# Last mixture-of-experts layer: tokens grouped before the experts, four experts a tile instead of eight

## What is computed

```python
flat = layernorm(h) * ln_scale + ln_bias              # 8768 x 128
out_shared = swiglu(flat @ shared_in_w.T) @ shared_out_w.T + shared_out_b
g_idx = argmax(flat @ group_gate_w.T + group_bias)    # one of 2 groups for each token
e_sel = expert logits of that group + bias            # 4 logits
e_probs = softmax(e_sel); topv, topi = top_k(e_probs, 2); topv /= topv.sum() + 1e-8
comb, cnt = zeros(S, 8), zeros(S, 8)                  # topv and 1.0 at g_idx*4 + topi
h_expert = swiglu(flat @ expert_in_w.T)               # 8768 x 256, the same for all experts
routed = cnt @ expert_out_bias
for e in range(8):
    routed += comb[:, e:e+1] * (h_expert @ expert_out_weight[e].T)
h = h + out_shared + routed
```

## Time and profile before

| | us |
|---|---|
| median of three runs | 1777.07 (1775.9 to 1777.42) |
| the profiled execution, its own time | 1775.86 |
| its span, first to last instruction | 1773.9 |
| `last_norm` | about 1345 to 1393 |
| `mix_experts` | 1393.98 to the end |
| mean granted clock of TensorE over the span | 0.902 |

### The profile page before, as it was taken

How to read it: one execution, slowest core, us unless ns; L and a number is a source line. 1 busy time by engine, 2 the same in 40 slices (tenths; PEclk the granted TensorE clock), 3 DMA queues, 4 the chain that set the end, 5 groups by cost and what they waited for, 6 DMA issues and landing times. The chain is left out here.

```text
span 1773.9 us, 27554 instructions
## 1 busy us (share of the span) xinstructions
PE 1388.5 (78%) x9068; PEld 992.5 (56%) x9068; DVE 1134.5 (64%) x1837; ACT 677.5 (38%) x1150; POOL 800.8 (45%) x833
## 2 busy tenths in 40 slices
PE   5679999999873332876727848888998699999998
PEld 3567777777542221765625623333334478887877
DVE  2755555555367782211114888888885889888998
ACT  3234444444443321322203548787875311111111
POOL 1455445444320034888865237777743333232331
PEclk9889999999985565999867969999999899999999
DMA  4070000000001032544443000000001000000000
GB/s 168 1 289 15 0 0 0 0 0 0 0 1 26 1 102 64 100 78 86 78 106 128 1 2 2 1 0 0 0 1 40 1 9 13 13 13 13 9 13 17
DMA packets 56803, 61.75 MB, mean 35 GB/s; under 512 B 15507, under 2 KB 46577, under 8 KB 55425
## 3 DMA queue, kind: packets, MB, share of 16 engines
q1 hardware_dynamic: 40835, 49.69, 8.6%
q0 software_dynamic: 13888, 10.24, 4.2%
q10 hardware_dynamic: 2016, 1.00, 0.2%
HBM read 36.49 MB, written 25.59 MB: 35 GB/s over the span
## 5 line engine op out<-in xcount | busy, mean ns | idle before, releaser
L1946 PE MATMUL at_slot<-at_qm,at_ks 128*128 128x512 bf16 (+1 forms) x640 | 160.3, 384 | 19.5 <-DVE at_clip L2151 10.2
L502 PE MATMUL ga_kv<-ga_kern,ga_v 128*128 128x274 f32 x512 | 133.5, 403 | 13.5 <-ACT ga_kern L591 12.6
L2667 DVE TENSOR_REDUCE mx_routed<-mx_weighted 128x128 f32<-128x1024 f32 x69 | 138.1, 2001 | 2.4
L2625 POOL TENSOR_TENSOR mx_h_E<-mx_hid_E,mx_h_E 128x768 fp32r<-128x768 f32 x23 | 43.5, 1890 | 188.8 <-DVE mx_h_E L2657 188.8
L84 PE MATMUL mx_e<-ff_expert_out_high,mx_h_E 128*128 128x512 f32 x276 | 112.3, 407 | 10.7 <-DVE mx_weighted L2664 10.7
L2030 ACT ACTIVATE at_clip<-at_slot,at_four 128x1024 bf16<-128x1024 f32 (+1 forms) x96 | 106.9, 1113 | 32.1 <-PE at_slot L1946 30.3
L1429 POOL DMA_INDIRECT moe_sums<-ex_y,slot_sums x69 | 108.4, 1570 | 22.4 <-issue 20.3
L2151 DVE TENSOR_SCALAR at_clip<-at_slot 128x1024 bf16<-128x1024 f32 (+1 forms) x96 | 116.1, 1218 | 3.1 <-PE at_slot L1946 2.8
L502 PEld LDWEIGHTS ga_kv<-ga_kern,ga_v 128*128 128x128 f32 x512 | 92.2, 189 | 37.8 <-ACT ga_kern L591 16.8
L85 PE MATMUL mx_e<-ff_expert_out_low,mx_h_E 128*128 128x512 f32 x276 | 109.6, 397 | 0.0
L653 POOL TENSOR_TENSOR ga_rot<-ga_by_cos,ga_by_sin 128x274 f32<-128x274 f32 x64 | 48.6, 759 | 134.9 <-DVE ga_by_sin L697 134.9
(11 more groups left out here) (457 smaller groups left out, 3835.9 us busy)
## 6 DMA issues: line engine op xcount, KB each, us to landing
moe_sums<-ga_zeros SPq DMA_DIRECT2D x8, 1152.0 KB, 13.4
ar_rows<-moe_sums SPq DMA_DIRECT2D x34, 256.0 KB, 3.9
ex_down<-in_down SPq DMA_DIRECT2D x32, 192.0 KB, 2.5
token_rows<-ct_rows SPq DMA_DIRECT2D x17, 256.0 KB, 2.4
out_h<-H SPq DMA_DIRECT2D x22, 192.0 KB, 1.9
H<-in_text SPq DMA_DIRECT2D x1, 4096.0 KB, 21.4
patches<-in_patches SPq DMA_DIRECT2D x1, 1728.0 KB, 8.2
ga_sin<-in_sin SPq DMA_DIRECT2D x1, 1644.0 KB, 7.9
```

What stands on the lines that cost most here:

```text
L502: last = nc.tensor.matmul(kv[:, e, 0:HALF], v[p][:, mt + 2 * side, e * P:(e + 1) * P], kern[(p + g) % 2][:, side, :], start=mt == 0 and si ...
L1946: last = nc.tensor.matmul(to[r0:r0 + r, g % 2, :].rearrange("p (s n) -> p s n", s=2), ks[m][:, t * P:t * P + r], qm[m][:, 2 * g:2 * g + 2, ...
L2667: nc.vector.tensor_reduce(R[p][t][:], weighted[:].rearrange("p e d -> p d e"), AX.X, ALU.add).then_inc(reduced, 1)
```

## The change

The last layer is split in two phases.

`last_norm` gains one DMA: a DRAM table `by_group` of 70 x 128 rows of 133 floats (4.77 MB) is filled with zeros from an input of the same size, and SyncE waits for it before it leaves the block.

`route()` also works out for each token a row of that table: tokens of the first group count up from the front, tokens of the second group count down from the back, with at least 64 blank rows between, so that every tile of 128 rows holds one group only. TensorE counts the tokens that come earlier (`rank`), and turns all 69 tiles of `F` to rows (`stage_turn`); ScalarE copies them to `stage` (`keep_stage`), beside four expert weights and the token's number. GpSimd scatters the rows of each tile to the table, 69 indirect DMAs.

Phase 1, beside the scatter, still goes by 23 chunks of 384 tokens and does only the shared feed-forward and the expert biases. Its output is turned to rows (`turn_rows`, `keep_rows`) and stored to the output, which is now 8768 x 128. Phase 2 reads the table back, 18 chunks of 4 tiles (the last of 2), turns the rows, does the experts' hidden layer 512 tokens at a time, and for each tile only the four experts of its group: 6 matmuls of 512 columns, whose column offset is worked out in a register. VectorE weighs and adds the four results with four operations on 128 x 128, each of which needs the one before. GpSimd adds the rows to the output by an indirect DMA that accumulates, 70 in all. GpSimd does no arithmetic in `mix_experts` any more; VectorE makes all low parts. The loops are unrolled.

The core of the diff, new lines only where an old one is told above:

```diff
@@ last_norm, sync
+            sp.dma_start(grouped_d, x["blank"]).then_inc(blanked, 16)
...
+            sp.wait_ge(blanked, 16)
@@ mix_experts, sync
+            for c in range(CHUNKS):
+                sp.wait_ge(rows_out, c + 1)
...
+                sp.dma_start(out[at:at + whole * P, :].rearrange("(t p) d -> p t d", p=P), rows[c % 2][:, 0:whole, :]).then_inc(stored[c % 2], 16)
...
+            sp.wait_ge(grouped, 1)
+            for c, (t, n) in enumerate(CHUNKS2):
+                if c >= LOADS:
+                    sp.wait_ge(weighed, CHUNKS2[c - LOADS][0] + CHUNKS2[c - LOADS][1])
+                sp.dma_start(tiles[c % LOADS][:, 0:n, :],
+                             grouped_d[t * P:(t + n) * P, :].rearrange("(t p) d -> p t d", p=P)).then_inc(loaded[c % LOADS], 16)
@@ mix_experts, tensor
+            def project(c):
+                pe.wait_ge(hidden, c)
                 pe.wait_ge(f_low, c + 1)
...
+            def experts(c, i, first_count):
+                j = CHUNKS2[c][0] + i
+                if i == 0:
+                    pe.wait_ge(h_low2, c + 1)
+                if j >= 2:
+                    pe.wait_ge(weighed, j - 1)
+                tokens = slice(i * P, (i + 1) * P)
+                at = (((P * j + BEYOND - first_count) >> BEYOND_BITS) & 1) * 512
...
+            project(0)
+            for g in range(EARLY):
+                stage_turn(g)
+            rank()
+            for g in range(EARLY, len(FGROUPS)):
+                stage_turn(g)
+            turn_cnt(0)
+            for c in range(CHUNKS):
+                if c + 1 < CHUNKS:
+                    project(c + 1)
+                finish(c)
+                if c + 1 < CHUNKS:
+                    turn_cnt(c + 1)
+                if c > 0:
+                    turn_rows(c - 1)
+            turn_rows(CHUNKS - 1)
+            first_count = nc.tensor.value_load(boundary[0:1, 0:1], min_val=0, max_val=NT)
+            pe.wait_ge(rows_out, CHUNKS)
+            turn(0)
+            turn(1)
+            project2(0)
+            for c, (t, n) in enumerate(CHUNKS2):
+                for i in range(n):
+                    experts(c, i, first_count)
+                    if i == 0 and c < LAST2:
+                        project2(c + 1)
+                    if i == 1 and c + 2 <= LAST2:
+                        turn(c + 2)
@@ mix_experts, gpsimd
+            for t in range(TILES):
+                if t % 4 == 0:
+                    pool.wait_ge(staged, t // 4 + 1)
+                nc.gpsimd.indirect_dma_start(out=grouped_d, out_offset=bass.IndirectOffsetOnAxis(ap=place_i[:, t:t + 1], axis=0),
...
+            for j in range(GTILES):
+                pool.wait_ge(weighed, j + 1)
+                nc.gpsimd.indirect_dma_start(out=out, out_offset=bass.IndirectOffsetOnAxis(ap=ids[:, j:j + 1], axis=0),
+                                             in_=R[j % RING], in_offset=None, bounds_check=NT - 1, oob_is_err=False,
+                                             compute_op=ALU.add).then_inc(sent[j % RING], 16)
@@ mix_experts, vector
+            def weigh(c, i):
+                j = CHUNKS2[c][0] + i
+                dve.wait_ge(expert_done, j + 1)
+                if j >= RING:
+                    dve.wait_ge(sent[j % RING], 16 * (j // RING))
...
+                nc.vector.tensor_scalar(r, part(0), share(0), None, ALU.mult).then_inc(acc, 1)
+                for e in range(1, 4):
+                    accs[0] += 1
+                    dve.wait_ge(acc, accs[0])
+                    nc.vector.scalar_tensor_tensor(r, part(e), share(e), r, ALU.mult, ALU.add).then_inc(acc if e < 3 else weighed, 1)
...
+            tokens(0)
             route()
+            tokens(1)
+            hide(0)
+            for c in range(CHUNKS):
+                if c + 1 < CHUNKS:
+                    hide(c + 1)
+                if c + 2 < CHUNKS:
+                    tokens(c + 2)
+                add(c)
...
+            for c, (t, n) in enumerate(CHUNKS2):
+                for i in range(n):
+                    weigh(c, i)
+                    if i == 1 and c < LAST2:
+                        hide2(c + 1, 0)
+                        high_at[c + 1] = accs[0]
+                    if i == min(2, n - 1) and c < LAST2:
+                        hide2(c + 1, 1)
+                    if i == min(2, n - 1) and c + 2 <= LAST2:
+                        tokens_low2(c + 2)
```

More of the change, by code:

```diff
@@ L51 @@
 NEX = 8
+GT = 4
+GCH = GT * P
+GTILES = -(-(NT + P - 1) // P)
+GROW = P + 5
+BEYOND_BITS = 14
+BEYOND = 1 << BEYOND_BITS
+ID_BIAS = 20000
 BIAS_ROWS = NE + EXPAND // P
@@ L2464, in _, with mix_experts @@
                 turn(n)
-def mix_experts(nc, k, H, F, GL, high, low, out):
+def mix_experts(nc, k, x, H, F, GL, high, low, grouped_d, out):
     with ExitStack() as st:
@@ L2515, in _ @@
+        from_front, to_back, token_id = (order[:, P + n * TILES:P + (n + 1) * TILES] for n in (1, 2, 3))
+        ones = order[:, P + 4 * TILES:]
+        FGROUPS = [(t, min(4, TILES - t)) for t in range(0, TILES, 4)]
+        EARLY = 4
+        CHUNKS2 = [(t, min(GT, GTILES - t)) for t in range(0, GTILES, GT)]
+        LAST2 = len(CHUNKS2) - 1
         @block.sync
         def _(sp):
-            with sp.Fori(0, CHUNKS - 1) as c:
-                sp.wait_ge(added, 2 * c + 3)
-                sp.sem_inc(met, 1)
-                sp.dma_start(out[:, bass.ds(c * CH, CH)], H[:, bass.ds(c * CH, CH)]).then_inc(stored, 16)
@@ L2521, in _ @@
-            sp.wait_ge(added, 2 * (CHUNKS - 1) + 3)
-            sp.dma_start(out[:, (CHUNKS - 1) * CH:NT], H[:, (CHUNKS - 1) * CH:NT]).then_inc(stored, 16)
-            sp.wait_ge(stored, 16 * CHUNKS)
+            sp.dma_start(order[:], x["order"]).then_inc(order_in, 16)
+            for c in range(CHUNKS):
+                sp.wait_ge(rows_out, c + 1)
+                whole = min(CT, (NT - c * CH) // P)
+                at = c * CH
+                sp.dma_start(out[at:at + whole * P, :].rearrange("(t p) d -> p t d", p=P), rows[c % 2][:, 0:whole, :]).then_inc(stored[c % 2], 16)
+                rest = min(CH, NT - at) - whole * P
+                if rest:
+                    sp.dma_start(out[at + whole * P:NT, :], rows[c % 2][0:rest, whole, :]).then_inc(stored[c % 2], 16)
@@ L2590, in _, with turn_cnt, finish @@
-            loop(pe, body)
-            finish(CHUNKS - 1, 0)
+            def turn_cnt(c):
+                if c == 0:
+                    pe.wait_ge(counted, 3)
+                    pe.wait_ge(staged, len(FGROUPS))
+                else:
+                    pe.wait_ge(cnt_out, c)
+                for t in range(CT):
+                    last = nc.tensor.transpose(t_ps[0][0:NEX + 1, t * P:(t + 1) * P], cnt[:, CT * c + t, :], k["ident"][:])
+                last.then_inc(cnt_ps, 1)
+            def finish(c):
+                pe.wait_ge(h_low, c + 1)
+                pe.wait_ge(placed_at if c < 2 else added, 1 if c < 2 else c - 1)
+                for f in range(2):
+                    split_matmul(nc, e_ps[c % 2][:, 0:CH], (high["shared_out"][:, f, :], low["shared_out"][:, f, :]),
+                                 [part[:, f, 0:CH] for part in h[c % 2]], f == 0, False)
+                pe.wait_ge(cnt_out, c + 1)
+                nc.tensor.matmul(e_ps[c % 2][:, 0:CH], high["out_bias"][:], cnt_t[:], start=False, stop=False)
+                nc.tensor.matmul(e_ps[c % 2][:, 0:CH], low["out_bias"][:], cnt_t[:], start=False, stop=True).then_inc(y_done, 1)
@@ new lines, in project2 @@
+            def project2(c):
+                n = CHUNKS2[c][1] * P
+                pe.wait_ge(hidden2, c)
+                pe.wait_ge(f_low2, c + 1)
+                for ps, at in ((a_ps, 0), (b_ps, 2)):
+                    for f in range(2):
+                        cols = slice((at + f) * P, (at + f + 1) * P)
+                        last = split_matmul(nc, ps[:, f, 0:n], (high["expert_in"][:, cols], low["expert_in"][:, cols]),
+                                            [part[:, 0:n] for part in f_parts[c % 2]], True, True)
+                last.then_inc(projected2, 1)
@@ new lines, in experts @@
+            def experts(c, i, first_count):
[6 more added lines that the diff above has]
+                at = (((P * j + BEYOND - first_count) >> BEYOND_BITS) & 1) * 512
+                for f in range(2):
+                    cols = bass.ds(at, 512)
+                    last = split_matmul(nc, e_ps[j % 2][:], [part[:, f, tokens] for part in h[c % 2]],
+                                        (high["expert_out"][:, f, cols], low["expert_out"][:, f, cols]), f == 0, f == 1)
+                last.then_inc(expert_done, 1)
@@ L2849, in _arrays @@
     a["owner"] = np.stack([~late, late], 1).astype(f)
+    token = np.arange(NTP).reshape(TILES, P).T
+    real = token < NT
+    front = np.where(real, token, 1 << 20)
+    back = np.where(real, GTILES * P - 1 - token, 0)
+    above = np.zeros((P, TILES))
+    above[:TILES] = np.arange(TILES)[:, None] < np.arange(TILES)[None]
```

(2 more changed lines are left out.)

367 lines of the change are left out of this document (195 added, 172 removed).

## The result

The changed kernel takes 1841.7 us, the median of four runs (1836.9 to 1842.2), beside 1777.2 us of the kernel before on the same chip: a ratio of 1.0358, with an interval of 1.0340 to 1.0377. The direction was forecast and the size was not: +64 us where the chain gave +26.

A forecast was written before the change was run, and what follows sets the result against it. TensorE (96.8% busy) and VectorE (90.4%), both nearly full, bound the last stage; a chain of fill, route, 23 chunks, handover, 18 chunks and end, with 2 us for cold starts, gave a span of 1800, hence 1803; range 1772 to 1842.

The forecast's parts named there:

- the chain: Whole span: fill, route, 23 chunks, handover, 18 chunks, end; 1800 against 1773.9, so 1803; 1790 to 1826 had 0.55.
- Removed and added work, and the transfers: Last stage: 12 matmuls a tile become 6, reductions vanish; fill 11.6 us and scatter 129 us, both hidden.
- Route and phase 1: From routing to the last `hide`: first `hide` at 1415, 21 rounds of 6.9 us, 145 us, last at 1564.
- Handover: Between the phases: from last `hide` to first expert matmul at 1584, 20 us in which no engine is full.
- Phase 2, the step that failed: Experts' phase: rounds of 12.2 us (bounds 11.3 and 14), 16 rounds 195 us, the short one 9.3.
- TensorE's clock: Both phases: new gaps of 2.5 and about 3 us lie near the 2.59 us wait, so full clock is kept.
- a part of it: Cold bursts in part: a quarter of phase 2's bursts gives +23, 1826; half of all +69, 1872; called likelier.
- the whole burst at half clock: Cold-bursts rival, both phases: 2.0 and 5.5 us a round, 137 us, 1940; colder or dearer rounds above 1826 had 0.20.
- The offset: Phase 2's round: 12.1 us taken as 12.2 for register work on the column offset, which no row prices.
- End: After the last chunk starts at 1788.5: last two tiles and last scatter, about 9 us, to 1797.7.
- VectorE's own rate: Rival, phase 2: weigh 1 not held up by TensorE's order, 10.1 us a chunk, 1769; 0.14, shared with other shorter rounds.
- no other order: Phase 2's two lists as they stand: the argument against VectorE's own rate, which would save 2.1 us a chunk.

The follow-up runs named there:

- the constant offset: Changed kernel with the experts' column offset a constant per tile (tiles 0 to 34 first group, rest second) instead of a register's value; 1827.3 us.
- the register ahead: Changed kernel with each tile's column offset written into a register ahead of the waits, one register instruction staying behind them; 1833.1 us, ratio 1.0304.
- the two lists: Changed kernel reordered: phase 1's VectorE splits tokens before the hidden layer, 1787.4 us; phase 2's TensorE projects two chunks ahead, VectorE's order following, 1779.6 us.

## Why the forecast was wrong

**Removed and added work, and the transfers.** Right. Columns halved, reductions gone; the fill landed in 20.2 us (11.6 forecast) and was hidden, the scatter took 1.32 us a tile (90.9 us for 69; 1.87 forecast as an upper bound) and was done at 1502.8, not 1540.

**Route and phase 1.** The first `hide` began at 1414.2 (1415), the undisturbed round is 6.78 us (6.9), each step as priced. But 21 rounds took 150.1 us (145), because five of them were 1.0 to 1.9 us longer, with matmuls at half clock. The last `hide` began at 1570.2 (1564): +6.

**Handover.** 23.8 us (20). The first projection ran at half the clock behind a wait of 4.81 us: 4.83 us from first to last start for its twelve matmuls instead of 2.68, which is 2.2 of the 3.8 us. First expert matmul at 1593.9 (1584): +10 so far.

**Phase 2, the step that failed.** Under "TensorE's clock" the forecast read one wait of 2.59 us with the clock up and 5.05 us with it down, found the new gaps near the first, and kept the sum at full clock. The run has gaps of 2.74 us, and in every round 7 or 8 matmuls behind the gap are at half clock: 1.5 us a round, 16 x 1.5 = 24 us, and 23 us of phase 2 came back when only the gap was filled. The step took a gap's length alone as the sign of what the clock does. The traces show that it isn't enough: in the kernel before, gaps of 2.17, 2.14 and 2.59 us within 14 us cost nothing (clock 1.00 from 785 to 820), phase 1 here has rounds with and without slow matmuls behind gaps of the same 2.08 us, and with the constant offset and with the register ahead two rounds each stayed at full clock behind 2.74 us. The right reading was its own rival, "a part of it": 1826 for a quarter of the loss.

The Trainium skill, "TensorE: Matmul & The Clock Gate", section "HAM oscillation", says that in its kernel each burst behind a wait starts cold. The trace agrees for phase 2 only in part: each burst has a stretch at half clock, of 7 or 8 x 0.43 = 3.0 to 3.4 us, but the earlier half of the bursts start at full clock and fall after one to five matmuls; in phase 1 it holds for five of 21 rounds. The forecast's use of it, the whole burst at half clock (5.5 us a round), is 3.6 times too dear.

**The offset.** It was given 0.1 us in place of a row. It cost 0.4 (0.44 against 0.04 with the constant offset) once a round, which both experiments confirm (-0.39 and -0.31 us a round): +5 us over phase 2 beyond the forecast.

Step by step the round of 1664.08 is, forecast in brackets: 24 matmuls 6.98 (5.5), to VectorE 0.43 (0.4), weighing 1.42 (1.5), multiplication 1.25 (1.25), copy 0.61 (0.70), weighing 1.42 (1.5), subtraction with the seam 1.67 (1.27). That is 13.78, where the sum was 12.12 and 12.2 was taken.

**End.** 12.3 us from the last chunk's first matmul at 1828.1 (9, and 2 for cold starts).

Together: +6.2 to the last `hide`, +3.8 handover, +26.7 in sixteen rounds and +3.0 in the short one, +0.8 at the end: 40 us over the forecast's span of 1800, 1840. Of the 26.7 about 24 are the clock behind the 2.74 us waits; the offset and a first round of 15.0 us, whose matmuls began at half clock behind the handover, make up the rest, less what the other steps took back.

**The rivals.** "VectorE's own rate" had its mechanism and its place right: 10.27 us is what the phase runs at once TensorE's order doesn't hold up the weighing (10.1 forecast). It did not happen because the lists are as they stand, and the forecast found "no other order" without trying one. The cost of that is now known: the two lists are 54 and 62 us, the clock's share in them included, more than the whole loss of 64.

**Left open.** What starts or ends the standstills. Two chips of the five had them, in all eight traces while GpSimd's scatters of phase 1 were issued or within 8 us of their end. That the scatter causes them was not shown, since neither kernel without it met such a chip. Nor is it shown what sets the place of a half-clock stretch in a round, or why five rounds of phase 1 had one here and one in others (1 to 5 in seven kernels with this list).

## To carry to other kernels

When a change replaces two full engines by a chain of dependent steps, the order inside the two lists is the change's price: write down for each engine what it is waiting for at each step, and move whatever is ready earlier ahead of it, before judging the algorithm. Here the same work was 3.6% slower in one order and 2.8% faster in another, on chips without standstills. A gap in TensorE that comes back in each round can cost more than itself, and should be priced by what follows it; even work that nobody reads can be worth putting there. An edit to an expression that holds a register may not move a single instruction: compare the instruction order before a run is read as a test of it.

## What the hardware showed unexpectedly

A gap of 2.74 us in each round of 13.8 us brought 7 or 8 matmuls at half clock in every round, often only after one to five at full clock. With the same gap two rounds of sixteen stayed at full clock in each of two other kernels; three gaps of 2.1 to 2.6 us in an earlier stage cost none, gaps of 2.08 us in phase 1 cost something in some rounds and nothing in most, and gaps of 0.5 to 0.8 us in each round cost none. A matmul with a register in its address, behind a wait, starts 0.44 us after the producer's end, 0.14 with all but one of the register instructions ahead of the wait, and 0.04 with a constant address. On two chips of five TensorE, VectorE and ScalarE stood still together for up to 32 us at a time while 69 indirect transfers were issued, and a kernel that took 1727 us elsewhere took 1811.
